# Cross-attention and feed-forward block: keys used as they are projected, scores and maxima in pairs on the upper and lower rows of the array

## The reference

```
q = layernorm(x) @ Wq + bq ;  k = ctx @ Wk + bk ;  v = ctx @ Wv + bv        (16 heads)
scores = q . k / sqrt(8) ;  scores[mask == 0] = -1e9                        (mask [32,1,56,1500], int32)
x = x + (softmax(scores) @ v) @ Wo + bo
h = gelu(quant_act(layernorm(x)) @ quant_weight(w1)) ;  x = x + quant_act(h) @ quant_weight(w2)
```

## Time and profile before

| | |
|---|---|
| median of 3 runs | 1034.27 us (1033.56 to 1036.57) |
| span of the profiled execution | 1031.0 us |
| TensorE matmul busy | 957.8 us (93%), x10188 |
| TensorE weight loads busy | 765.4 us (74%) |
| VectorE busy | 776.9 us (75%) |
| ScalarE busy | 645.0 us (63%) |
| GpSimd busy | 252.6 us (24%) |
| DMA, mean | 119 GB/s |
| mean granted TensorE clock | 0.981 of full speed |

### The profile page before, as it was taken

How to read it: one execution, slowest core, us unless ns; L and a number is a source line. 1 busy time by engine, 2 the same in 40 slices (tenths; PEclk the granted TensorE clock), 3 DMA queues, 4 the chain that set the end, 5 groups by cost and what they waited for, 6 DMA issues and landing times.

```text
span 1031.0 us, 29506 instructions
## 1 busy us (share of the span) xinstructions
PE 957.8 (93%) x10188; PEld 765.4 (74%) x10188; DVE 776.9 (75%) x1796; ACT 645.0 (63%) x1176; POOL 252.6 (24%) x414
## 2 busy tenths in 40 slices
PE   4688999999999999999999999999999999999994
PEld 2366787887878787787878778787877878787772
DVE  4688777777877877787787778788777868878753
ACT  2155567676676757666676766667676666767572
POOL 6223132222202222220222222021222212122200
PEclk9689999999999999999999999999999999999997
DMA  5763266554545655554565554456655545664400
GB/s 132 169 146 83 69 148 147 121 133 113 119 113 137 145 127 133 121 117 105 130 145 133 131 126 116 106 123 145 140 127 127 118 107 119 142 143 107 106 2 5
DMA packets 74985, 123.09 MB, mean 119 GB/s; under 512 B 6016, under 2 KB 58960, under 8 KB 74960
## 3 DMA queue, kind: packets, MB, share of 16 engines
q1 hardware_dynamic: 73097, 121.58, 51.3%
q10 hardware_dynamic: 1863, 1.17, 0.4%
HBM read 37.22 MB, written 0.92 MB: 37 GB/s over the span
## 4 chain that ended last, share of the span: by engine, by line
PE 60%; DMA 12%; DVE 12%; SPq 8%; issue 5%; ACT 3%; DVEq 0%; ACTq 0%
PE ps_v L808 11%; DMA keys<-k_lo 10%; PE ps_s L764 10%; PE ps_s L769 10%; PE ps_p L720 9%; SPq L366 8%; PE ps_p L701 6%; PE ps_p L705 6%; DVE keys L942 3%; DVE seg_max L978 2%; PE ps_p L698 2%; PE ps_p L713 2%; ACT probs L614 1%; DVE recip L1011 1%; PE ps_p L715 1%
## 5 line engine op out<-in xcount | busy, mean ns | idle before, releaser
L614 ACT ACTIVATE probs<-ps_s 125x448 f32<-125x448 f32 x768 | 379.8, 546 | 183.8 <-PE ps_v L808 95.8
L978 DVE TENSOR_REDUCE seg_max<-ps_p 128x1 f32<-128x500 f32 x672 | 424.2, 673 | 50.0 <-PE ps_p L720 34.7
L764 PE MATMUL ps_s<-qry,keys 121*125 121x448 f32 x768 | 306.8, 407 | 5.5 <-ACT probs L614 5.4
L769 PE MATMUL ps_s<-qry,keys 128*125 128x448 f32 x768 | 275.9, 373 | 0.0
L720 PE MATMUL ps_p<-keys,qry 120*128 120x500 f32 x576 | 212.9, 430 | 22.5 <-DVE k_lo L965 12.6
L530 POOL TENSOR_TENSOR q_hi<-q_flag,ones_f 64x56 fp32r<-64x56 f32 x64 | 19.0, 296 | 659.0 <-DVE q_flag L972 656.5
L764 PEld LDWEIGHTS ps_s<-qry,keys 121*125 121x125 f32 x768 | 142.2, 188 | 49.8 <-ACT probs L614 21.8
L808 PE MATMUL ps_v<-probs,vals 125*32 125x112 f32 x6144 | 167.1, 260 | 0.7 <-ACT probs L614 0.7
L808 PEld LDWEIGHTS ps_v<-probs,vals 125*32 125x32 f32 x6144 | 144.0, 110 | 25.8 <-issue 17.9
L769 PEld LDWEIGHTS ps_s<-qry,keys 128*125 128x125 f32 x768 | 142.5, 189 | 27.2 <-issue 10.3
L720 PEld LDWEIGHTS ps_p<-keys,qry 120*128 120x128 f32 x576 | 109.9, 193 | 51.8 <-DVE k_lo L965 16.1
(11 more groups left out here) (123 smaller groups left out, 779.6 us busy)
## 6 DMA issues: line engine op xcount, KB each, us to landing
keys<-k_hi SPq DMA_DIRECT2D x128, 375.0 KB, 6.9
keys<-k_lo SPq DMA_DIRECT2D x64, 375.0 KB, 7.7
ctx_sb<-in_ctx_dram SPq DMA_DIRECT2D x31, 750.0 KB
keys<-keys SPq DMA_DIRECT2D x32, 328.1 KB
mask_sb<-in_mask_Bx1xSxS_ik_dram SPq DMA_DIRECT2D x31, 328.1 KB
out_dram<-x_rows SPq DMA_DIRECT2D x16, 56.0 KB, 1.6
ctx_sb<-in_ctx_dram ACTq DMA_DIRECT2D x1, 750.0 KB
x_rows<-in_x_dram SPq DMA_DIRECT2D x1, 672.0 KB, 9.8
```

The source lines that it names most:

```text
L614: act.activation(probs[:, c % NP, h], ps_s[0:KC, j % NS, 0:HC], ACT.Exp).then_inc(exp_done, 1)
L764: return pe.matmul(ps_s[0:KC, (2 * c + h) % NS, 0:HC], keys1[0:ONE + 1, p, h, c * KC:(c + 1) * KC], qry1[0:ONE + 1, p, h, :], start=start, ...
L769: return pe.matmul(ps_s[0:KC, (2 * c + h) % NS, 0:HC], keys2[:, p, h, c * KC:(c + 1) * KC], qry2[:, p, h, :], start=start, stop=not start)
L978: dve.tensor_reduce(seg_max[:, m, s:s + 1], bank[:, 0:SEG], AX.X, ALU.max)\
```

## The change

The keys are used where the projection leaves them, 128 rows for 16 heads, two batches deep; the eight placements are gone. A score is four products for each half of the heads, and the halves lie on rows 0 to 63 and 64 to 127 of the array, with outputs in different banks: k_hi.q_hi, k_lo.q_hi, k_hi.q_lo, and mask and shift (57 rows). That is 96 matmuls of 448 columns a batch. `S`, `s`, `f` now mean a whole chunk of both halves (12 a batch), and ScalarE takes two exponentials at each. `M` is 8 pairs of heads x 3 segments, 24 matmuls on 64 rows, neighbours on upper and lower rows; VectorE adds the mask while it takes the maximum. The mask bias comes in three pieces on 121 rows, the mask is loaded twice, to rows 0 and 64, the shift goes out in two DMAs. GpSimd prepares the queries in 4 operations instead of 12. `vals` is double, `probs` holds 12 chunks instead of 6. Both lists are written anew; in them maxima come in groups of four, `sum` and `some` are neighbours, `G0` stands ahead of `K0`.

```diff
-COUNT = {"T": 3, "K": 3, "F": 1, "V": 3, "M": 21, "R": 1, "D": 1}
+COUNT = {"T": 3, "K": 3, "F": 1, "V": 3, "M": NM, "R": 1, "D": 1}
 EVEN = order("""
-    own T0 s0 s1 s2 D0 f0 T1 f1 f2 M0 S3 M1 M2 S4 M3 M4 S5 S6 S7 M5 S8 sum M6 S9 M7 M8 O0 rows S10
-    T2 M9 S11 k0 K0 S12 M10 S13 P0 M11 S14 M12 S15 M13 M14 S16 some P1 M15 M16 M17 M18 S17 F0 S18 K1
-    M19 S19 S20 k1 M20 neg V0 K2 R0 S21 S22 k2 bias S23 V1 V2 rows1 P2
+    own s0 T0 T1 D0 f0 M0 M1 M2 M3 S1 V0 O0 S2 T2 M4 M5 M6 M7 S3 rows S4 K0 k0 M8 M9 M10 M11 S5 V1 bias0
+    P0 S6 sum some F0 M12 M13 M14 M15 S7 V2 S8 K1 k1 rows1 M16 M17 M18 M19 S9 P1 bias1 S10 M20 M21 M22 M23
+    S11 neg K2 k2 R0 bias2 P2
 """)
 ODD = order("""
-    s0 s1 own s2 T0 T1 f0 f1 M0 f2 M1 M2 M3 S3 H0 S4 S5 M4 S6 S7 M5 sum M6 M7 S8 S9 M8 T2 M9 K0 G0
-    S10 k0 M10 M11 P0 hid M12 hid1 S11 D0 S12 K1 M13 k1 S13 S14 M14 K2 hid2 S15 S16 hid3 M15 S17 S18
-    S19 k2 U0 M16 S20 S21 M17 S22 M18 M19 M20 neg P1 Y0 R0 S23 some bias V0 F0 V1 P2 V2
+    own s0 T0 T1 D0 f0 M0 M1 M2 M3 S1 V0 H0 S2 T2 M4 M5 M6 M7 S3 G0 S4 K0 k0 M8 M9 M10 M11 S5 V1 bias0 hid
+    P0 S6 sum some F0 hid1 M12 M13 M14 M15 S7 V2 hid2 S8 K1 k1 hid3 M16 M17 M18 M19 S9 U0 P1 bias1 S10 Y0 M20 M21 M22 M23
+    S11 neg K2 k2 R0 bias2 P2
 """)
-NP = 6
+NP = NC
...
+                for at in (0, SLOT):
+                    sp.dma_start(mask_sb[at:at + SQ, p, :], src).then_inc(mask_loaded[p], 16)
...
-                for h in range(2):
-                    copy(keys1[0:HR, p, h, :], k_hi[HR * h:HR * (h + 1), :]).then_inc(keys1_placed[p][h], 16)
-                sp.wait_ge(mask_biased, b + 1)
-                copy(keys1[HR:ONE, p, 1, :], keys1[HR:ONE, p, 0, :]).then_inc(keys1_placed[p][1], 16)
-                for h in range(2):
-                    copy(keys2[0:HR, p, h, :], k_hi[HR * h:HR * (h + 1), :]).then_inc(keys2_hi_placed[p], 16)
-                for h in range(2):
-                    copy(keys2[HR:128, p, h, :], k_lo[HR * h:HR * (h + 1), :]).then_inc(keys2_lo_placed[p], 16)
...
+                    s, j = divmod(n, NPAIR)
+                    r, h = divmod(j, 2)
+                    rows, a = slice(SLOT * h, SLOT * (h + 1)), 2 * r
+                    mm = pe.matmul(bank[0:MROWS, 0:SEG],
+                                   qry_hi[rows, p, a:a + 2, :].rearrange("p a q -> p (a q)")[:, 0:MROWS],
+                                   k_hi[rows, p, s * SEG:(s + 1) * SEG], start=True, stop=True)
...
+            def score(bt, c, first, last):
...
+                products = [(hi, q_hi_of, HR), (lo, q_hi_of, HR), (hi, q_lo_of, HR),
+                            (bias, own_query[:, p, :, :], SQ + 1)]
+                for n in range(first, last):
+                    key, query, rows = products[n]
+                    for h in range(2):
+                        part = slice(SLOT * h, SLOT * h + rows)
+                        mm = pe.matmul(ps_s[0:KC, (2 * c + h) % NS, 0:HC].rearrange("k (a q) -> k a q", a=HH),
+                                       key[part, :], query[part], start=(n == 0), stop=(n == 3))
+                return mm
...
+            def open_score(bt, c):
...
+                wait(pe, exp_done, 2 * (NC * b + c) - 1)
+                score(bt, c, 0, 3)
...
-                dve.tensor_scalar(keys1[HR:ONE, p, 0, :], mask_sb[HR:ONE, p, :], 0.0, -BIG,
+                dve.tensor_scalar(mask_bias[0:MROWS + 1, p, at], mask_sb[0:MROWS + 1, p, at], 0.0, -BIG,
...
-                    dve.tensor_reduce(seg_max[:, m, s:s + 1], bank[:, 0:SEG], AX.X, ALU.max)\
+                    if j == 0:
+                        dve.wait_ge(mask_biased, NSEG * b + s + 1)
+                    wait_bank_full(dve, slot, how, st)
+                    dve.sem_inc(seg_begun, 1)
+                    dve.tensor_tensor_reduce(max_junk[0:MROWS, BANK[how][slot], :], bank[0:MROWS, 0:SEG],
+                                             mask_bias[0:MROWS, p, s * SEG:(s + 1) * SEG].bitcast(F32), 1.0, LOWEST,
+                                             ALU.add, ALU.max, seg_max[0:MROWS, 4 * h + r, s:s + 1])\
                         .then_inc(seg_done, 1)
...
+                    if kind in ("S", "f"):
+                        exp(bt, 2 * n)
+                        exp(bt, 2 * n + 1)
```

More of the change, by code:

```diff
@@ L33 @@
 NT = B * SQ // PAIR
+NGRP = 4
 BIG = float(2 ** 30)
+LOWEST = -3.0e38
 MAGIC = 1.5 * 2 ** 23
@@ L91, in ahead_only @@
     return [slot for slot in base if AHEAD.get(slot[0], 0) in ahead]
-LEAD = "T0 T1 T2 " + " ".join(f"M{n}" for n in range(21)) + """ neg R sum some F K0 k0 K1 k1 K2 k2
-    V0 V1 V2 bias"""
+LEAD = "T0 T1 T2 " + " ".join(f"M{n}" for n in range(NM)) + """ neg R sum some F K0 k0 K1 k1 K2 k2
+    V0 V1 V2 bias0 bias1 bias2"""
 PASS = {
-    "open": order("T0 T1 T2 X0 Q0 Q1 sum some F K0 k0 K1 k1 K2 k2 bias"),
+    "open": order("T0 T1 T2 X0 Q0 K0 k0 K1 k1 K2 k2 sum some F bias0 bias1 bias2"),
     "lead": order(LEAD),
-    "first_even": with_more(EVEN, {"s1": "norm1", "S5": "X1 norm2", "S7": "Q2", "S9": "Q3 abs", "S11": "B", "k1": "X2", "S21": "Q4", "S23": "Q5",
-                             "M20": "Z"}, ahead=(0, 1, 2)),
-    "first_odd": with_more(ODD, {"s1": "norm3", "S5": "W0", "S7": "W1", "S11": "X3", "k1": "Q6", "S21": "Q7"}),
+    "first_even": with_more(EVEN, {"S1": "norm1", "S2": "X1 norm2", "S3": "Q1", "S4": "abs", "S5": "B", "K1": "X2", "S10": "Q2",
+                             "M23": "Z"}, ahead=(0, 1, 2)),
+    "first_odd": with_more(ODD, {"S1": "norm3", "S2": "W0", "S3": "W1", "S5": "X3", "K1": "Q3"}),
     "even": EVEN,
@@ L727, in fill @@
                 elif kind == "Q":
-                    g, h = divmod(n, 2)
-                    mm = pe.matmul(bank[:, 0:4 * PAIR], wq_sb[:, h].rearrange("p a n -> p (a n)"),
-                                   xnt[:, g % 2, :], start=True, stop=True)
+                    mm = pe.matmul(bank[:, 0:4 * PAIR], wq_sb[:], xnt[:, n % 2, :], start=True, stop=True)
                 elif kind == "Z":
@@ L796, in values, with close_score @@
+            def close_score(bt, c):
+                b, k, p = bt
+                if c == 0:
+                    pe.wait_ge(shift_placed[p], 32 * (k + 1))
+                if c == 0 and isinstance(b, int) and b < 2:
+                    pe.wait_ge(filled, 4)
+                if c % NG == 0:
+                    pe.wait_ge(mask_biased, NSEG * b + c // NG + 1)
+                score(bt, c, 3, 4).then_inc(scores_ready, 1)
             def values(bt, n):
@@ L961, in take @@
                     dve.wait_ge(k_hi_ready, NSEG * b + n + 1)
-                    if n == 0:
-                        wait(dve, keys2_lo_placed[1 - p], 32 * (k + p))
                     at = slice(n * SEG, (n + 1) * SEG)
-                    dve.scalar_tensor_tensor(out=k_lo[:, at], in0=bank[:, 0:SEG], scalar=bk_sb[:, 0:1],
-                                             in1=k_hi[:, at].bitcast(F32), op0=ALU.add, op1=ALU.subtract)\
+                    dve.scalar_tensor_tensor(out=k_lo[:, p, at], in0=bank[:, 0:SEG], scalar=bk_sb[:, 0:1],
+                                             in1=k_hi[:, p, at].bitcast(F32), op0=ALU.add, op1=ALU.subtract)\
                         .then_inc(k_lo_ready, 1)
```

260 lines of the change are left out of this document (102 added, 158 removed).

## The result

Over four runs of each on one chip the changed kernel takes 1423.78 us (1423.23 to 1425.48) and the one before 1035.17 us: ratio 1.376, 95% interval 1.3739 to 1.3782. The forecast was 1342 with a range of 1230 to 1460. The sign and the range held. The size was off by 82 us, and 1424 lies above the forecast's own range of 1240 to 1420: it will be seen that the time came out by the mechanism of the clock rival, to which the prediction gave 0.14.

The account below looks back on a forecast made before the run. TensorE's issue was taken to bound the kernel before (28.7 of 29.9 us a batch), the order of waits the changed one: 30 x 10.3 = +309, lead -2, from 1031.0 to 1338, as run median 1342; range 1230 to 1460.

Parts of the forecast that it names:

- the clock rival: TensorE's waits at F0, M11 and M19 halve its clock each step: 2 to 4 us more, 1400 to 1460; chance 0.14.
- The walk: Both loop lists followed once through the engines' waits from the last product of P2: 40.0 us even, 40.5 odd.
- Mean 40.2: Mean length of the loop's even and odd steps after the change: 40.2 us, 10.3 more than 29.9.
- The new maximum: VectorE's maximum with the mask added: 0.73 us each, bounds 0.63 to 0.92, 17 of 24 on the path.
- 37.2 to 43.5 us a step: Range of a loop step from the maximum at 0.63 or 0.92 us and switches at half price.
- worth nearly nothing inside the loop: Removing the key placements (DMA, 12% of the chain) gains nearly nothing, as they run beside a TensorE that hardly idles.
- TensorE's own sum: TensorE's work per batch after the change: 24.8 us without switches of array shape, 29.3 with 22.5 at 0.2 each.
- The switches eat the halved maxima: On TensorE, 14.5 more shape changes cost 1.6 to 3.1 us, against a gain of 2.4 from scores and maxima.
- The bare mask chain: S6, exponentials, mask sum, some, F0, M12 form one chain in each step; TensorE does nothing for 3.3 us of it.
- Pairs not side by side: Row halves of score products do not overlap: a chunk takes 1.64 us, +4.5 a step, about 1480; chance 0.05.
- Waits that cover each other: Loop waits overlap better than walked, only the mask-sum chain is bare: 33.2 us a batch, 1133; chance 0.11.
- The other side: Half-row shape switches are free and VectorE keeps ahead: TensorE needs 28.1 us a batch, 980; chance 0.05.

Follow-up runs that it names:

- run 2: Changed kernel with 13 unread half-row matmuls per loop step put into F's bank ahead of the wait for some_diag: 1380.67 us, ratio 1.3373.
- run 6: Changed kernel with ScalarE's mask sum moved in both lists from behind S6 to behind T2: 1274.10 us, ratio 1.2323.
- run 5: Kernel before, with each key placement copy moving 8 columns instead of the whole row from the third batch on: 1008.53 us, ratio 0.9757.
- run 11: run 7's kernel with one small matmul added per score chunk, on all rows in even steps, on rows 0 to 63 in odd ones: 1153.31 us, ratio 1.1173.
- run 7: Changed kernel, same operations, both lists reordered: mostly one to three maxima between chunks, sum, some and F apart, gelu early in the odd step: 1063.40 us, ratio 1.0298.
- run 8: As run 7 with a second such order, F ahead of S8 (even) and K0 (odd), chunks and maxima mixed otherwise: 1065.81 us, ratio 1.0317.
- run 4: Changed kernel with the maximum taken by a plain reduce, the mask not added: 1426.05 us, ratio 1.3791.
- run 3: Changed kernel with a score chunk's loops over halves and products exchanged, three products of one half, then three of the other: 1425.58 us, ratio 1.3804.

## Why the forecast held where it did, and where it failed

**The walk.** Its times, from the last product of P2, against the trace. The walk's 23.1 and 24.6 include the first maximum behind F, and in the odd step hid1; the table has F's own end from its terms:

| | forecast, even / odd | even | odd |
|---|---|---|---|
| k0 taken | 14.2 / 15.5 | 14.5 | 16.2 |
| F0 done | 22.5 / 23.8 | 22.8 | 27.1 |
| k1 taken | 28.6 / 30.1 | 30.8 | 35.1 |
| end of P2 | 40.0 / 40.5 | 40.2 | 45.1 |

The even step was right up to F. The step of the prediction that missed is "Mean 40.2": 42.7 was measured, and 30 x 2.45 = 74 of the missing 82 us are this. **The clock** was left out of that sum and kept as a rival at 0.14; it occurred. Pieces of the odd step's chain at the 1.2 GHz level are S 1.49, V 2.00, P 2.32 (below), V 2.05, S 1.52, which against 0.82, 1.07, 1.67, 1.07, 1.02 is 3.7 us; in the even one V 2.00 and S 1.64 make 1.6. The mean of 2.7 lies inside the rival's "2 to 4 us more per step", and 1424 inside its 1400 to 1460. Runs 2 and 6 confirm the mechanism: where TensorE has work in the wait at F, or no wait there, the same pieces are back at 1.07 to 1.14 and 1.00. I had the lead's maxima at half clock in front of me and waits of 3.3 us in my own walk, and should have given that case the larger chance.

Everything else nearly cancelled, and that is luck. **The new maximum** was taken as 0.73 and is 0.60. The walk has 17 of them on its path; in the trace 12 stand in the even step's chain and 4 in the odd one's, so it was 8 x 0.13 = 1.0 us a step too much, not 2.2. rows1 was entered with the 3.06 us of the trace before and stood for about 2 on the path, in the even step alone. The other way, the stretches up to k0 were longer by 0.3 and 0.7 us, though the maxima in them are shorter: TensorE's slots from M0 to T2, and not the maxima, end last there. Behind F the walk enters the first maximum twice (0.63 and 0.73) and leaves out S7 (0.8), which is nearly the same: from F's end to k_hi it has 4.7 us, the trace 6.5, and 1.5 to 1.6 of that are the clock.

The ranges do not hang together either: 37.2 to 43.5 us a step is 1252 to 1441 by the forecast's own 30 steps, not 1240 to 1420. The 42.7 lies inside the first and 1424 outside the second. The chain of the odd step behind the wait for k0:

```profile
801.79 0.75 DVE k_lo L915
...
802.58 0.77 PE ps_p L669
803.35 1.49 PE ps_s L722 x8
804.84 2.00 PE ps_p L661 x8
806.84 2.32 PE ps_v L757 x64
```

**What bounds the kernel, and the placements.** TensorE's issue bounding the kernel before held in kind, but "worth nearly nothing inside the loop" failed: 25 us (run 5), 1.0 us a batch in the loop. The wait of k_lo for the copies stands in the earlier trace rows, 48.2 us over the run; the prediction gave it no cost, but once in two batches it reached TensorE.

**TensorE's own sum.** 24.8 without and 29.3 with changes of shape was forecast. Pairs at 0.20 to 0.21 held. A change measured 0.14 to 0.16 in run 11 and about 0.2 at the borders in the trace, inside "0.11 to 0.21". By the counting that gives run 7's 25.5 and the 8 of before, in which P is a shape of its own, the changed kernel has 24.5 changes a step, not 22.5, which adds 0.4 us. Run 7, where nothing else bounds, measured 30.0 for 25.5 changes; the forecast's own terms give 24.8 + 25.5 x 0.16 = 28.9, and 29.9 at 0.2. "The switches eat the halved maxima" held.

**The order.** That the order, not the work, makes the loss held: runs 6 to 8. The bare mask chain came as told, some_diag ahead of F and ScalarE's mask sum directly ahead of it, 94 us in all for 32 x 3.3 = 106 forecast. Gelu with its two table loads ahead of K0 delayed k0 of the odd step by 1.7 us against the even one (1.3 forecast).

**The signs.** The waits named came as told, pairs start under 0.02 us apart and follow after 0.20, and the DMA share is 0.13. Two signs missed: the new maximum, 0.60, lies below "0.63 to 0.92", and TensorE is busy for 587 of 720 us in the loop, 81% and not under 75%. At the lower clock the same matmuls are busy for longer: 34.8 us a step, 29.3 forecast.

**The rivals.** Clock: occurred, under-weighed. Pairs not side by side: out. Waits that cover each other, 1133: not in this order, but run 7 is that case brought about. The other side, 980 with free changes: out, since a change is not free and the best of three orders stays 3% above the kernel before. The change as a whole, where the order doesn't stand in the way, then: 2.4 us a batch less for the pairs, 17.5 more changes at 0.16 to 0.2, so 2.8 to 3.5 more, together 31 x 0.4 to 1.1 = 12 to 34 us more, and 25 less for the placements. Run 7 should be between 13 us under the kernel before and 9 us above it, and it is 29 above. TensorE's busy time a batch grew from 29.0 (29.9 x 698 / 720) to 30.0, which the 0.4 to 1.1 of these terms cover at the upper price. What stays open is 20 to 42 us. Shown of it are 0.3 us a batch by which TensorE idles more in run 7 than in run 5 (0.4 and 0.1), and about 9 us outside the loop: the two runs are 55 us apart, the loop's 30.4 and 29.0 us a batch give 46 of them. For the rest, maxima parted from their partner, 12 in run 7's two steps, and waits counted as busy are candidates that no run separates. No version here beats the kernel before.

## What to carry to other kernels

When engines take an order strictly, price a new order by walking it, and look for an operation of a little used engine that stands between two waits of the bound engine: a 1.4 us slot, moved by a few places, was worth 150 us here. Where that walk has TensorE idle in each step for as long as it was here (3.0 to 3.2 us), put the half clock behind it into the sum rather than among the rivals. And splitting matmuls into row halves that run side by side halves them only where half-row work stays together: count the changes of shape, at 0.14 to 0.2 us each here, before counting the gain.

## What the runs showed of the hardware unexpectedly

- A maximum over 500 columns with an add of a second operand, one operand in PSUM and one in SBUF, follows itself every 0.60 us, its accumulator read included; the plain reduce does so every 0.59 (run 4).
- Half-row matmuls that the kernel's text has three and three ran as pairs of opposite halves, 0.20 us a pair (run 3).
- A small half-row matmul of 8 columns put among half-row pairs cost 0.00 us in the chunk shown and 0.07 a chunk over its step, and the same on all rows 0.41 and 0.39 (run 11).
- The half clock began 1.9 us after the end of a 3.0 us wait at F, with TensorE at work in between, and at once behind the 3.2 us wait for k0 of the odd step (changed kernel).
